# Holding a support matrix in two float32r parts instead of three bfloat16 ones, in a two-layer graph kernel on one core

## The reference

```
support = x @ W0                                  # 64x64 weights
rank = cumsum(adj != 0, axis=1); deg = rank[:, -1:]
k = minimum(deg, 100); pos = rank - (deg - k)
w = mask * where(pos > 0, 0.5 ** (k - pos), 0)    # halves with each later neighbour
x = layernorm(x + w @ support + b0)

h = (adj @ x + x) / (rowsum(adj) + 1)
z = relu(concat([x, h]) @ W1 + b1)
x = layernorm(x + z / max(norm(z), 1e-12))
```

## Time and profile before

| | |
|---|---|
| median of 3 runs | 111.45 us |
| the profiled execution | 110.99 us |
| its span, first to last instruction | 109.2 us |
| PE busy in the span | 91.9 us |
| DVE / ACT / POOL busy | 61.3 / 58.0 / 18.8 us |

### The profile page before, as it was taken

How to read it: one execution, slowest core, us unless ns; L and a number is a source line. 1 busy time by engine, 2 the same in 40 slices (tenths; PEclk the granted TensorE clock), 3 DMA queues, 4 the chain that set the end, 5 groups by cost and what they waited for, 6 DMA issues and landing times.

```text
span 109.2 us, 2379 instructions
## 1 busy us (share of the span) xinstructions
PE 91.9 (84%) x876; PEld 73.7 (67%) x876; DVE 61.3 (56%) x186; ACT 58.0 (53%) x126; POOL 18.8 (17%) x44
## 2 busy tenths in 40 slices
PE   0349299999999999999999999999999999996000
PEld 0248068777777777777676676678988999995000
DVE  1003527564525247899998402226378339999991
ACT  0602644396665656666648886633214208479640
POOL 6200000000000142200074200000000000367870
PEclk9999999999999999999999999999999999999955
DMA  2999999799999999999799910000000000000224
GB/s 61 297 300 349 373 388 369 252 393 388 385 388 388 384 389 385 386 378 202 169 213 212 115 28 0 6 0 0 0 6 0 0 0 0 6 0 0 48 53 94
DMA packets 22314, 20.23 MB, mean 185 GB/s; under 512 B 13600, under 2 KB 14624, under 8 KB 22304
## 3 DMA queue, kind: packets, MB, share of 16 engines
q1 hardware_dynamic: 22144, 20.06, 61.2%
q10 hardware_dynamic: 160, 0.03, 0.1%
HBM read 17.47 MB, written 0.52 MB: 165 GB/s over the span
## 4 chain that ended last, share of the span: by engine, by line
PE 72%; DVE 13%; DMA 4%; ACT 4%; issue 3%; SPq 1%; DVEq 0%
PE acc L869 18%; PE cnt L856 13%; PE cnt L858 12%; PE tmp L837 10%; PE acc L900 7%; PE cnt L900 5%; DMA stage<-in_adj_dram 4%; PE tmp L888 3%; DVE stats L438 3%; DVE t L571 3%; ACT wts L324 2%; PE acc L914 2%; DVE t L582 1%; PE tmp L879 1%; PE tmp L914 1%
## 5 line engine op out<-in xcount | busy, mean ns | idle before, releaser
L324 ACT ACTIVATE wts<-cnt 128x512 int16<-128x512 f32 x64 | 37.8, 597 | 23.1 <-PE cnt L858 22.8
L869 PEld LDWEIGHTS acc<-sup,wts 128*128 128x128 bf16 x256 | 22.9, 98 | 13.5
L869 PE MATMUL acc<-sup,wts 128*128 128x192 bf16 x256 | 31.2, 246 | 0.0
L533 DVE COPY adjT<-tmp 128x1024 bf16<-128x1024 bf16 x24 | 16.5, 688 | 20.9 <-PE tmp L837 20.9
L856 PE MATMUL cnt<-adjT,rest 128*128 128x512 bf16 x60 | 22.8, 380 | 2.3 <-ACT wts L324 2.2
L858 PE MATMUL cnt<-adjT,suffix 128*128 128x512 bf16 x64 | 24.5, 383 | 0.0
L837 PE MATMUL tmp<-ident,stage 128*128 128x128 bf16 x192 | 15.5, 227 | 1.9 <-DMA stage<-in_adj_dram 1.9
L275 POOL TENSOR_TENSOR adjT<-adjT,ident 128x128 bf16<-128x128 bf16 x16 | 7.3, 487 | 49.9 <-PE cnt L858 49.9
L837 PEld LDWEIGHTS tmp<-ident,stage 128*128 128x128 bf16 x192 | 13.1, 102 | 3.0 <-issue 2.5
L900 PE MATMUL acc<-ysp,adjT 128*128 128x194 bf16 x128 | 12.4, 247 | 0.0
L900 PEld LDWEIGHTS acc<-ysp,adjT 128*128 128x128 bf16 x128 | 11.0, 98 | 0.2
(11 more groups left out here) (98 smaller groups left out, 83.8 us busy)
## 6 DMA issues: line engine op xcount, KB each, us to landing
stage<-in_adj_dram SPq DMA_DIRECT2D x15, 1024.0 KB, 14.0
stage<-in_adj_dram SPq DMA_DIRECT2D x4, 256.0 KB, 4.4
xs<-in_x_dram SPq DMA_DIRECT2D x2, 256.0 KB, 5.7
out_dram<-xs SPq DMA_DIRECT2D x3, 128.0 KB, 2.0
out_dram<-xs SPq DMA_DIRECT2D x2, 64.0 KB, 1.7
wd<-in_L_gnn_W_dram SPq DMA_DIRECT2D x4, 16.0 KB, 8.3
adjT<-nat SPq DMA_TRANSPOSE x4, 5.4
wd<-in_L_gnn_weight_dram ACTq DMA_DIRECT2D x2, 16.0 KB, 4.0
```

What stands on the lines that cost most here:

```text
L324: nc.scalar.activation(wts[:, c, n % WRING, :].bitcast(I16), cnt[:, c, :], ACT.Relu).then_inc(w_ready[c], 1)
L533: nc.vector.tensor_copy(adjT[:, q, bp // 2, :, bp % 2 * 2:bp % 2 * 2 + 2, :], bank.bitcast(BF16).rearrange("p (r k n) -> p r k n", r=RT, k ...
L869: last = nc.tensor.matmul(acc[:, c * RT + r, 0:PD], wts[:, c, n % WRING, r * P:(r + 1) * P], sup[:, b, :], start=(b == NB - 1 and r % 2 == ...
```

## The change

`sup` becomes two parts in float32r (a 32-bit format that PE takes as one operand), 128 columns wide. [...] ACT's Relu still writes int16, now into a ring `w16` of 2 per chain, and POOL copies each 128x512 tile into `wts`, now float32r with a ring of 3. Weigh waits for POOL's copy. The sums afterwards run over two parts.

At the head, PE gets six matmuls of zeros before the transposition of x and four behind it. The copy of xT goes from ACT to DVE. Two steps of the support's split fall away for each half. The calls for m = 5 and m = 6 change places on PE and DVE. The addition of `b0` to x (L525) comes six ticks earlier. POOL's 16 identity additions are put between its copies, at ticks 16, 18, 25 and 27. `PIECES` writes the packs down row by row, but in the places where they were. Scratch tiles are shared so that all fits.

```diff
-WRING = 4
+WRING = 3
+SRING = 2
+ORDER = (0, 1, 2, 3, 4, 6, 5) + tuple(range(7, TICKS))
+WARM = (6, 4)
+DIAG_AT = (16, 18, 25, 27)
...
-        wts = sb("wts", [P, 2, WRING, CH], BF16)
+        w16 = sb("w16", [P, 2, SRING, CH], BF16)
+        wts = sb("wts", [P, 2, WRING, CH], F32R)
-        sup = sb("sup", [P, NB, PD], BF16)
+        sup = sb("sup", [P, NB, SD], F32R)
...
+            def widen(c, n):
+                pool.wait_ge(w_ready[c], n + 1)
+                if n >= WRING:
+                    pool.wait_ge(w_used[c], n - WRING + 1)
+                nc.gpsimd.tensor_copy(wts[:, c, n % WRING, :], w16[:, c, n % SRING, :]).then_inc(w_cast[c], 1)
...
+            for tick in range(TICKS):
+                if tick < STEPS:
+                    widen(0, tick)
+                if tick >= BEHIND:
+                    widen(1, tick - BEHIND)
+                for q in range(Q):
+                    if tick == DIAG_AT[q]:
+                        diagonal(q)
...
-            act.wait_ge(xT_done, 1)
-            nc.scalar.copy(xT[:, 4:8, :], acc[:, 2:4, :].rearrange("p a (b n) -> p (a b) n", n=P)).then_inc(xT_ready, 1)
             act.wait_ge(sup_done, 1)
             nc.scalar.activation(sup[:, PT:NB, 0:D], ...
-            act.wait_ge(sup_left, 1)
-            nc.scalar.copy(sup[:, PT:NB, D:2 * D], left32[:, PT:NB, :]).then_inc(sup_mid, 1)
...
-                if n >= WRING:
-                    act.wait_ge(w_used[c], n - WRING + 1)
-                nc.scalar.activation(wts[:, c, n % WRING, :].bitcast(I16), cnt[:, c, :], ACT.Relu).then_inc(w_ready[c], 1)
+                if n >= SRING:
+                    act.wait_ge(w_cast[c], n - SRING + 1)
+                nc.scalar.activation(w16[:, c, n % SRING, :].bitcast(I16), cnt[:, c, :], ACT.Relu).then_inc(w_ready[c], 1)
...
-                    sums = acc[:, c * RT:(c + 1) * RT, 0:PD].rearrange("p t (k d) -> p t d k", k=PARTS)
+                    sums = acc[:, c * RT:(c + 1) * RT, 0:SD].rearrange("p t (k d) -> p t d k", k=2)
...
-                if m == ENDS[0] - 1:
+                if m == ENDS[0] - 7:
...
-                pe.wait_ge(w_ready[c], n + 1)
+                pe.wait_ge(w_cast[c], n + 1)
...
-                    last = nc.tensor.matmul(acc[:, c * RT + r, 0:PD], wts[:, c, n % WRING, r * P:(r + 1) * P],
+                    last = nc.tensor.matmul(acc[:, c * RT + r, 0:SD], wts[:, c, n % WRING, r * P:(r + 1) * P],
...
+            def warm(n):
+                zeros = w16[:, 0, 0, :]
+                for _ in range(n):
+                    nc.tensor.matmul(cnt[:, 0, :], zeros[:, 0:P], zeros, start=True, stop=True,
+                                     skip_group_check=True)
+
+            pe.wait_ge(warm_set, 1)
+            warm(WARM[0])
             pe.wait_ge(ident32_ready, 1)
             transpose_x(1, acc_bank(2)).then_inc(xT_done, 1)
+            warm(WARM[1])
```

More of the change, by code:

```diff
@@ L10 @@
 PD = PARTS * D
+SD = 2 * D
 CH = 512
@@ L45 @@
 F32 = mybir.dt.float32
+F32R = mybir.dt.float32r
 BF16 = mybir.dt.bfloat16
@@ L111, in build @@
         wd_zeroed = sem("wd_zeroed")
+        warm_set = sem("warm_set")
         zeroed = sem("zeroed")
@@ L127, in build @@
         w_ready = [sem(f"w_ready{i}") for i in range(2)]
+        w_cast = [sem(f"w_cast{i}") for i in range(2)]
         w_used = [sem(f"w_used{i}") for i in range(2)]
@@ L174, in build @@
         fills = []
-        for m in range(TICKS):
+        for m in ORDER:
             if m == XT0:
@@ L269, in _, with diagonal @@
             nc.gpsimd.memset(ysp[:, :, PD:PD + 2], 1.0).then_inc(consts, 1)
-            for q in range(Q):
+            def widen(c, n):
[3 more added lines that the diff above has]
+                nc.gpsimd.tensor_copy(wts[:, c, n % WRING, :], w16[:, c, n % SRING, :]).then_inc(w_cast[c], 1)
+            def diagonal(q):
                 pool.wait_ge(cnt_done[q % 2], min(step(q, RT * q) + 2, (q // 2 + 1) * NB))
@@ L339, in y_middle @@
                 act.wait_ge(y_left, q + 1)
-                nc.scalar.copy(ysp[:, rows(q), D:2 * D], left32[:, rows(q), :]).then_inc(y_mid, 1)
+                nc.scalar.copy(ysp[:, rows(q), D:2 * D], t0[:, rows(q), :]).then_inc(y_mid, 1)
             for tick in range(TICKS):
@@ L480, in finish_layer0, with pack @@
                     dve.wait_ge(y_mid, q + 1)
-                    nc.vector.tensor_tensor(ysp[:, v, 2 * D:3 * D], left32[:, v, :], ysp[:, v, D:2 * D],
+                    nc.vector.tensor_tensor(ysp[:, v, 2 * D:3 * D], t0[:, v, :], ysp[:, v, D:2 * D],
                                             ALU.subtract).then_inc(y_ready, 1)
-            def pack(i):
+            def pack(i, r):
                 u = len(units) - TURNED + i
-                wait_adj(dve, u)
-                for r in range(RT):
-                    nc.vector.tensor_copy(nat[:, i, r, :], stage[:, u % RING, r, :]).then_inc(nat_ready, 1)
+                if r == 0:
+                    wait_adj(dve, u)
+                nc.vector.tensor_copy(nat[:, i, r, :], stage[:, u % RING, r, :]).then_inc(nat_ready, 1)
+            nc.vector.memset(w16[:, 0, 0, :], 0.0).then_inc(warm_set, 1)
             nc.vector.memset(square[:, 0:1], 1.0).then_inc(table_fed, 1)
@@ L493, in _ @@
             nc.vector.memset(wd1[:], 0.0).then_inc(wd_zeroed, 1)
[L494 removed]
+            dve.wait_ge(xT_done, 1)
+            nc.vector.tensor_copy(xT[:, 4:8, :], acc[:, 2:4, :].rearrange("p a (b n) -> p (a b) n", n=P)).then_inc(xT_ready, 1)
+            for m in ORDER:
                 if m == 2:
                     dve.wait_ge(sup_hi, 1)
[L497 removed]
+                    nc.vector.scalar_tensor_tensor(out=sup[:, PT:NB, D:SD],
                                                    in0=acc[:, 6:8, :].rearrange("p a (b d) -> p (a b) d", d=D),
[L499 to L504 removed]
+                                                   scalar=SUP_SCALE, in1=sup[:, PT:NB, 0:D].bitcast(F32),
+                                                   op0=ALU.mult, op1=ALU.subtract).then_inc(sup_ready, 1)
                 if m == XT0:
@@ L535, in _ @@
                         tmp_read[number[("adj", q, bp)] % 2], 1)
-                for i in range(TURNED):
-                    if m == PACKS[i]:
-                        pack(i)
+                for i, r in PIECES.get(m, ()):
+                    pack(i, r)
             for q, part in ((2, 0), (2, 1), (2, 2), (2, 3), (2, 4), (3, 0), (3, 1), (3, 2), (3, 3), (3, 4), (2, 6), (2, 7),
@@ L940, in _ @@
                     weigh(0, tick - LAG)
-                m = tick + LEAD
+                m = ORDER[tick + LEAD] if tick + LEAD < TICKS else tick + LEAD
                 if m == XT0:
```

25 lines of the change are left out of this document (5 added, 20 removed).

## The result

The changed kernel takes 115.85 us (median; 114.83 to 116.85) beside 111.81 us for the kernel before on the same chip: ratio 1.0337, 95% interval 1.0231 to 1.0444. Medians are of all executions of a kernel, while ratios leave out those that ran in a slower state. The changed kernel is slower by 3.4%, where 108.1 us had been forecast. The profiled execution of the change took 115.93 us with a span of 114.2; that of before had 110.99 and 109.2, so 5.0 us of span have to be found.

The account below looks back on a forecast made before the run. PE's own work was taken as the bound from 20 to 91 us, with DVE as tight around m = 20 to 26. Gains of 1.8 us up to tick 26 and 1.8 - 0.3 behind gave 107.7 profiled, 108.1 median; range 104.8 to 115.0.

Parts of the forecast that it names:

- The weigh: PE's group of four 128-column float32r matmuls: 0.25 us per group, 0.08 less than before.
- the head: Kernel start: first Relu near 9.2 us, some 2.5 us sooner, with at most 1.75 us gained by tick 11.
- the stretch at DVE: m = 20 to 26, DVE without a gap: sharing with POOL costs 1.6 us, leaving 1.8 us gained at tick 26.
- The rule of the Trainium skill: Weight loads on PE: no fast load for FP32, an estimated 107 ns for 128 columns, which would make the sum slower.
- Rival B: Slower: a 32-bit weight load of 0.112 us bounds each float32r matmul, weigh 0.48 us, median 118.5 us; chance 0.13.
- middle of B: Weight load of middle length on PE: matmul 0.098 us, weigh 0.42 us, median 114.7 us; chance 0.06.
- the tick-11 load: Load that PE's call at tick 11 waits for: lands at 28.4 us, so at most 1.75 us is gained by then.
- Moving L525 six ticks ahead: Earlier addition of b0 on DVE: changes nothing in the stretch m = 20 to 26, since it lay before.
- POOL: Widening copies at 0.55 us each (0.5 to 1.5): POOL keeps up, but slows DVE from m = 21 to 24.
- C: Slower: POOL is the bound, at 1.1 us per copy a tick takes 0.4 us more, 122 us; chance 0.04.
- After tick 25: Later weighs on PE: 23 at 0.08 us less save 1.8 us, minus 0.3 in ticks 32 to 34.
- E: Slower: float32r at full float32's price, 0.93 us per weigh, 38 us more, 149 us; chance 0.03.

Follow-up runs that it names:

- e1: Separate kernel without the computation: groups of matmuls by type and width, then POOL copies and DVE casts alone and together; a 128-column float32r matmul costs 0.11 us.
- e7: Changed kernel with only the support's high part streamed, 64 columns per float32r matmul: 117.21 us, ratio 1.0238.
- e8: Changed kernel with two support blocks streamed at once, 256 columns per float32r matmul: 119.86 us, ratio 1.0682.
- e11: Changed kernel without the ten matmuls of zeros: 115.48 us, ratio 1.0345.
- e12: Changed kernel measured again, with nothing altered: 115.17 us, ratio 1.0339.
- e10: Changed kernel with the addition of b0 put back to its old place: 116.85 us, ratio 1.0461.
- e3: Changed kernel with the old head: no zero matmuls, ACT copies xT, calls in order, b0 added at its old place; 118.47 us, ratio 1.0602.
- e9: Changed kernel with each weigh's operands exchanged: support block as weights, 512 columns streamed, one matmul instead of four; 111.02 us, ratio 0.9947.

## Why the prediction was wrong

**The weigh: the step that failed.** "I take one pass and one cycle per column: as long as a bfloat16 one of 128 columns, 0.056 us." One pass and one cycle per column are both right (e1, 256 records, 0.229 us at 512 columns). It is wrong that this sets the price at 128: a float32r matmul there costs 0.11 us (e1), the distance between the starts of two 32-bit weight loads, and a weigh is 0.40 to 0.41 instead of 0.25. 51 weighs that were to save 4.1 us cost 4.1 more, which is 8.2 of the 8.3 us between the forecast's span and the measured one. The other errors cancel: the head brought 1.7 us less than forecast, the stretch at DVE took 0.5 less, and 0.9 more than forecast was hidden at the end. The distances in the earlier trace rows, 0.115 against 0.22, didn't speak against it: at two cycles per column 256 columns take longer than a load and 128 take about as long as one, so the shorter of the two widths couldn't tell columns from load. The prediction said so, and I chose the reading that suited the sum. The rule of the Trainium skill ("TensorE: Matmul & The Clock Gate", LDWEIGHTS) that the prediction set beside it, an estimate of 107 ns for a load of 128 columns, was the better guide; e1 gives 0.112 to 0.113 us up to 192 columns.

**Rival B was the mechanism**, at 0.40 instead of 0.48, since nothing is added for entering from bfloat16: four at 0.112 are 0.45, and measured around the group they are less (the estimate under e7 and e8). B's own sum, 118.5, had the weigh too dear. I had given nearly that price, 0.42, to a "middle of B" with 114.7 us, and a chance of 0.06. That it came close to 115.85 is partly luck: it had 1.3 us of gain in the head that didn't come, and no hold at DVE. The range ended at 115.0.

**The head.** The zeros took the clock to its upper level and the first Relu came at 8.53 us (forecast 9.2). That the loads let little of it through was right, but the sum had 1.75 us at tick 11 and 0.1 came: the tick-11 load, 14.3 us after its issue, lands at 29.9, not 28.4. Its landing moves the end one for one. In the changed kernel, e11 and e12 tick 11's count starts at 30.70, 30.52 and 31.02, and the last one at 80.99, 80.83 and 81.32, 50.3 us later each time. So the forecast took the landing of one execution for a fixed time. "Moving L525 six ticks ahead changes nothing here" was wrong: it was worth 2.0 us between tick 11 and the last count (e10).

**POOL.** 0.56 us alone for a forecast of 0.55, 0.65 as a mean in the kernel; it is never the bound, so C falls. That it slows DVE in the stretch of m = 20 to 26 was right in place. The size agrees by luck: I put 1.6 us on DVE, and PE's hold is 1.44 + 0.16 us, but DVE itself lost some 3.2 us up to 60 us, 2.4 of them in the 16 casts, of which only the first part reached PE. And I had set the loss against a gain on PE, and there was none: it came on top.

**After tick 25** the forecast had 23 x 0.08 as a gain less 0.3; they were 0.08 dearer each, and of the dearer weighs 0.6 is hidden at the end. E never came near: the records are one per matmul.

## What to carry to other kernels

Price a float32r matmul as the longer of its columns and a floor, which here is 0.11 us with weights of 128x128: below some 250 columns fewer columns save next to nothing (0.03 us of a weigh when they are halved), and the wide operand should stream past the narrow one (0.24 us against 0.40 for the same products). Before work is put on an idle POOL, ask what DVE does at that time: its casts and two-input operations between SBUF tiles can be held up. And where PE is held for longer than now, look at the granted clock behind the hold: in e10 0.7 us more of hold brought 1.6 us of lower clock with it. And where one price in a sum has two readings, weight them by what the rows exclude, not by which of them makes the change pay.

## What I had not expected of the hardware

- By starts, a float32r matmul is priced 0.112, 0.113, 0.113, 0.120, 0.174 and 0.229 us at 64, 128, 192, 256, 384 and 512 columns: a floor, then one cycle per column at 2.4 GHz. Using the same weights again doesn't lower it.
- POOL and DVE exclude each other in two ways. Behind 16 casts without a gap a POOL copy stood for 5.8 us while DVE lost nothing (e1). Inside the kernel they took turns: four casts in 2.95 us instead of 1.42, 0.75 apart, with POOL's copies between them. Operations on four elements a partition were hit as well, 0.53 instead of 0.16 us. What decides between the two ways was not tried.
- Raising TensorE's clock ahead of time with zeros moved the first Relu by 1.4 us and the end by nothing (e11).
- A hold of PE can cost twice. After 2.13 us (e10, e3) and 3.5 us (e9) without work the granted clock fell to 0.50 for some microseconds; after 1.44 us (changed kernel, e11, e12) it stayed at 1.00.
